# Per-batch weight loads into a ring of three, and four column strips of the array for the first conditioning step

## The chip, the cores and the metric

The kernel runs on one core of one Trainium2 chip. The metric is the device time of one execution in microseconds (us), median of several runs. A core has TensorE (PE in the rows; PEld is its weight load), VectorE (DVE), ScalarE (ACT), GpSimd (POOL) and SyncE (SP), which here does nothing but issue DMA transfers.

## What is computed

Two layers on 128 batches of 32 tokens of 128 features, fp32. Each layer is a conditioning step, chosen by an id of the batch, and a mixture of experts. The change touches the first conditioning step alone:

```python
def _L0_cond_ref(x, subjects, weights, b):        # weights: (16, 128, 128)
    w = weights[subjects]                         # one 128 x 128 matrix per batch
    out = jnp.einsum('bnc,bcd->bnd', x, w)
    out = out + b[subjects][:, None, :]
    return out
...
x = x + _L0_ffn_ref(_L0_cond_ref(x, itok_B_0_15, ...), ...)   # 16 experts, top 1, and a shared expert
x = x + _L1_ffn_ref(_L1_cond_ref(x, itok_B_0_8, ...), ...)    # adapter and norm; 8 experts, top 2, shared
```

So each 32 tokens (one batch) are multiplied by one of 16 matrices, and which one is known only when the ids have been read.

## The kernel before

The 4096 tokens are `NG` = 8 token tiles of 512 (`GP`). A tile is `G` = 4 groups of 128 tokens, and a group is `QB` = 4 batches of `S` = 32 tokens. Every engine has a program of its own; semaphores tie them. The first stage goes through the 8 tiles, software-pipelined, in the loop `for n in range(NG + 1)` of PE (line 1165), ACT (607) and DVE (806). On PE one turn n is, in this order:

1. `x_in(n + 1)`: four transposes of the next tile's x into `PS[0]`; ACT copies them to `xT` (line 604).
2. four transposes of tile n-1's conditioned rows `condS` (a view of `t3`) into `PS[5]`; DVE adds the bias and writes `featT` (line 810).
3. the 16 batch products of tile n (lines 1183 to 1192). All 16 matrices lie in SBUF in `c0w`, fetched once by ACT's queue (line 598). PE loads 16 offsets of the tile into its registers (`values_load...`, TENSOR_LOAD, line 1183) and reads the matrix of each batch at a register's offset (line 1189). The stationary operand is the 128 x 32 piece of `xT`. Batch b of a group goes to bank `PS[1 + b]`, partitions 0 to 31, so that there are four banks, and four copies of 32 x 512 move them to the right quarter of `condS`: two by ACT (line 613), two by DVE (line 817).
4. the router's logits of tile n-1 (line 1206), and four transposes back into token rows (`PS[7]`), which ACT copies to `disp` (line 617).

After every second tile DVE finds the best expert of each token (`first_max`, lines 795 to 799). After the last, DVE scans the counts (line 850), PE ranks the tokens (lines 1236 to 1239), DVE computes `slot`, and POOL scatters the 32 groups of rows to DRAM (`rows0`, line 536). It starts only when `rows0` has been filled with zeros (semaphore `zero0`, line 529). SP fetches the first blocks of it back (line 418) when all scatters have landed (`sc0`), and the experts begin.

SP issues its transfers in one fixed order: x of tiles 0 and 1, ids, five small tables (line 374), x of the other six tiles, the shared expert's weights (377 to 379; PE waits for them as `ld_sh0`, line 1232), eight loads of the experts' `w_raw` (line 382), twelve zero fills of `rows0` (388), `w_dn` (390), 28 zero fills for layer 1 (393, 396), layer 1's tables (400 to 411), and then the wait for `sc0`. ACT and POOL split `w_raw` into two parts as the tiles go by (lines 619 to 623, 523 to 527).

Of the kernel before, what the change touches and what calls it, by code (L numbers as in the profile page):

```python
# [5 lines left out]
def adaln_moe_two_layers(  # L6
# [35 lines left out]
    ALU = mybir.AluOpType  # L42
    ACT = mybir.ActivationFunctionType
    AX = mybir.AxisListType
    ds = bass.ds
# [22 lines left out]
    G = 4  # L68
# [37 lines left out]
    with ctx:  # L106
# [35 lines left out]
        sw1h = sb("sw1h", [P, F1], fp32r)  # L142
        sw1l = sb("sw1l", [P, F1], fp32r)
        used = (2 * NG + 4 + 2) * GP + 10 * F1 + 2 * NX * ROW + 4 * H + 4 * GP + 2 * NCH * P
        sb("spare", [P, NSUB * H + E0 * (C0 * H + 2 * F0x2) - used])
# [20 lines left out]
        blk_x = [sb(f"blk_x{s}", [P, ROW]) for s in range(4)]  # L166

        act0, act1 = (a[:, C0:C1, :].rearrange("p c t -> p (c t)") for a in act)
        assert 4 * H + 2 * F0 <= (C1 - C0) * GP
# [70 lines left out]
        ld_small = sem("ld_small")  # L240
        ld_c0w = sem("ld_c0w")
        ld_tab = sem("ld_tab")
# [11 lines left out]
        dve_ready = sem("dve_ready")  # L254
        off_ready = sem("off_ready")
        pe_tab = sem("pe_tab")
# [4 lines left out]
        condA = sem("condA")  # L261
        condD = sem("condD")
        pe_ht = sem("pe_ht")
# [102 lines left out]
        def _(sp):  # L366
            sp.dma_start(acc[:, 0:G, :], x_g[0]).then_inc(x_ld[0], 16)
            sp.dma_start(w0off[:, :], subj).then_inc(ld_small, 16)
            sp.dma_start(acc[:, G:2 * G, :], x_g[1]).then_inc(x_ld[1], 16)
            sp.dma_start(subjI[:, :], subj.partition_broadcast(NSUB)).then_inc(ld_tab, 16)  # L370
            sp.dma_start(langI[:, :], lang.partition_broadcast(NLANG)).then_inc(ld_tab, 16)
            for dst, src in ((c0bs[:, :], c0_b), (gam[:, :], c1_gamma), (bet[:, :], c1_beta),
                             (rt0[:, :], f0_router), (rt1[:, :], f1_router)):
                sp.dma_start(dst, src).then_inc(ld_tab, 16)
            for g in range(2, NG):
                sp.dma_start(acc[:, g * G:(g + 1) * G, :], x_g[g]).then_inc(x_ld[g], 16)
            sp.dma_start(shg[:, :], f0_sh_gate).then_inc(ld_sh0, 16)
# [3 lines left out]
            for r in range(E0 // 2):  # L381
                sp.dma_start(w_raw[:, r * 2 * F0x2:(r + 1) * 2 * F0x2].rearrange("p (e f) -> p e f", e=2),
                             f0_gate_up[2 * r:2 * r + 2].rearrange("e p f -> p e f")).then_inc(g_ld[r], 16)

# [207 lines left out]
        def _(eng):  # L592
            sc = nc.scalar

            def cp(dst, src):
                return sc.activation(dst, src, ACT.Copy)  # L596

            eng.dma_start(c0w[:, :].rearrange("p (s h) -> p s h", s=NSUB),
                          c0_w.rearrange("s p h -> p s h")).then_inc(ld_c0w, 16)
            eng.preload_act_table(ACT.Sigmoid)  # L600
# [6 lines left out]
            for n in range(NG + 1):  # L607
                if n < NG:
                    if n + 1 < NG:
                        copy_x(n + 1)  # L610
                    for b in range(2):
                        eng.wait_ge(pe_c, QB * n + b + 1)
                        cp(condS[b * S:(b + 1) * S, :, :],
                           PS[1 + b][0:S, :].rearrange("p (i h) -> p i h", h=H)).then_inc(condA, 1)
                if n >= 1:
                    eng.wait_ge(pe_tok, n)
                    cp(disp[:, (n - 1) * G:n * G, 0:H],
                       PS[7][:, :].rearrange("p (i h) -> p i h", h=H)).then_inc(tok_done, 1)
# [143 lines left out]
        def _(dve):  # L762
# [14 lines left out]
            v.memset(a_b1[TAIL:LASTK, NCH - 1:NCH], 1.0).then_inc(dve_ready, 1)  # L777
            dve.wait_ge(ld_small, 16)
            v.tensor_scalar(w0off[:, :], w0off[:, :], float(H), None, ALU.mult).then_inc(off_ready, 1)
            dve.wait_ge(poolk, 19)  # L780
# [25 lines left out]
            for n in range(NG + 1):  # L806
                if n >= 1:
# [5 lines left out]
                                    ALU.add).then_inc(hT_done, 1)  # L813
                if n < NG:
                    for b in range(2, 4):
                        dve.wait_ge(pe_c, QB * n + b + 1)
                        v.tensor_copy(condS[b * S:(b + 1) * S, :, :],
                                      PS[1 + b][0:S, :].rearrange("p (i h) -> p i h", h=H)).then_inc(condD, 1)
                if n == 0:
# [323 lines left out]
        def _(pe):  # L1143
# [21 lines left out]
            for n in range(NG + 1):  # L1165
                if n + 1 < NG:
                    x_in(n + 1)
                if n >= 1:
                    pe.wait_ge(condA, 2 * n)
                    pe.wait_ge(condD, 2 * n)  # L1170
                    if n == 1:
# [6 lines left out]
                if n < NG:  # L1178
                    pe.wait_ge(xT_done, n + 1)
                    if n == 0:  # L1180
                        pe.wait_ge(ld_c0w, 16)
                        pe.wait_ge(off_ready, 1)
                    _, offs = nc.values_load_multi_w_load_instructions(
                        w0off[0:1, n * GB:(n + 1) * GB], engines=(mybir.EngineType.PE,), min_val=0,
                        max_val=(NSUB - 1) * H, skip_runtime_bounds_check_because="subjects are under NSUB")
# [356 lines left out]
```

## Time and profile before

| | |
|---|---|
| three runs | 533.38, 534.56, 535.95 us, median 534.56 |
| the profiled execution | 532.79 us, span 531.0 us, mean granted TensorE clock 0.939 |
| first stage, first to last batch product | 9.58 to 64.7 us |
| scatter of rows for layer 0 | 79.75 to 122.4 us |
| PE, DVE, ACT, POOL busy | 84%, 45%, 47%, 48% of the span |

The span runs from the first to the last instruction; 1.8 us lie around it. Times in the trace are from the span's start. A name ending in q (SPq, PEldq) is an engine's sequencer: register work and DMA issues. The granted clock is TensorE's share of full speed: 1.00 is 2.4 GHz, 0.50 is 1.2 GHz.

### The profile page before, as it was taken

The numbers are of one execution on the slowest core, as the hardware profiler recorded it, in microseconds if no ns is written. First come the engines' busy times: TensorE is split into PE (matmuls) and PEld (weight loads), VectorE is DVE, ScalarE is ACT, GpSimd is POOL, SyncE is SP. The second block draws the span as 40 slices with busy tenths as digits, with TensorE's granted clock in tenths as the row PEclk, the third lists the DMA queues.
The fourth block names the chain that finished last, engine by engine and source line by source line (L and its number), as shares of the span: only waits on it lengthen the run. The fifth ranks groups of instructions, "written<-read, shape, count | busy, mean of one in ns | idle before, by whom it ended". The sixth has DMA issues, their size and how long they took to land.

```text
span 531.0 us, 9984 instructions
## 1 busy us (share of the span) xinstructions
PE 447.7 (84%) x3129; PEld 384.3 (72%) x3130; DVE 240.2 (45%) x708; ACT 247.4 (47%) x593; POOL 256.3 (48%) x272
## 2 busy tenths in 40 slices
PE   6798879965999998899997879918999999999900
PEld 4698746644777775477786869908999999999800
DVE  1344486422555554244868865212333233323237
ACT  2234486202555553356456534403555555555424
POOL 3003567771555555500246777760555555655510
PEclk8989999996999999899999799977999999999965
DMA  9999921111322220800001111113234324331169
GB/s 255 398 308 356 393 63 45 55 50 46 78 71 68 78 64 8 237 10 2 11 30 42 45 51 46 55 40 100 66 116 123 107 68 141 109 79 34 35 175 307
DMA packets 66131, 57.96 MB, mean 109 GB/s; under 512 B 9485, under 2 KB 53152, under 8 KB 66099
## 3 DMA queue, kind: packets, MB, share of 16 engines
q1 hardware_dynamic: 58402, 43.99, 27.7%
q0 software_dynamic: 7168, 12.51, 7.3%
q10 hardware_dynamic: 528, 1.05, 0.5%
q8 instruction: 18, 0.29, 0.2%
q14 instruction: 15, 0.11, 0.1%
HBM read 30.28 MB, written 29.47 MB: 113 GB/s over the span
## 4 chain that ended last, share of the span: by engine, by line
PE 63%; POOL 12%; issue 12%; DVE 5%; DMA 5%; ACT 1%; POOLq 1%; SPq 0%; DVEq 0%; ACTq 0%
PE PS L1459 13%; PE PS L1145 8%; POOL rows L568 7%; PE PS L1189 6%; PE PS L1381 4%; POOL rows L536 4%; PE PS L1268 4%; PE PS L1447 4%; PE PS L1448 4%; PE PS L1449 4%; PE PS L1253 2%; PE PS L1255 2%; PE PS L1254 2%; PE PS L1368 2%; PE PS L1206 2%
## 5 line engine op out<-in xcount | busy, mean ns | idle before, releaser
L586 POOL DMA_INDIRECT back<-grp_y,grp_i x80 | 79.6, 996 | 71.9 <-DVE grp_y L1102 58.0
L568 POOL DMA_INDIRECT rows<-disp,slot x64 | 64.9, 1014 | 66.8 <-DVE slot L946 47.2
L1459 PE MATMUL PS<-w2r,act 128*128 128x128 f32 x640 | 77.7, 275 | 0.0
L1459 PEld LDWEIGHTS PS<-w2r,act 128*128 128x128 f32 x640 | 74.7, 191 | 0.0
L735 ACT ACTIVATE act<-PS,b1r 128x256 f32<-128x256 f32 x160 | 62.8, 475 | 14.5 <-PE PS L1449 14.5
L547 POOL DMA_INDIRECT back<-act,blk_i x48 | 47.0, 980 | 42.0 <-DVE act L906 21.3
L1102 DVE TENSOR_TENSOR grp_y<-PS,b2r 128x256 f32<-128x256 f32 x40 | 17.0, 425 | 89.3 <-PE PS L1459 84.4
L596 ACT ACTIVATE xh<-PS 128x256 fp32r<-128x256 f32 (+1 forms) x48 | 20.0, 418 | 74.2 <-PE PS L1145 74.2
L1447 PE MATMUL PS<-xh,w1h 128*128 128x256 f32 x160 | 48.3, 302 | 0.0
L526 POOL TENSOR_TENSOR w_gul<-w_raw,w_guh 128x512 fp32r<-128x512 f32 x16 | 21.0, 1336 | 50.1 <-ACT w_guh L596 50.1
L1448 PE MATMUL PS<-xl,w1h 128*128 128x256 f32 x160 | 44.9, 281 | 0.0
L1449 PE MATMUL PS<-xh,w1l 128*128 128x256 f32 x160 | 44.9, 281 | 0.0
L1189 PE MATMUL PS<-c0w,xT 128*32 x256 | 32.6, 291 | 7.3 <-issue 7.3
L536 POOL DMA_INDIRECT rows<-disp,slot x32 | 31.7, 990 | 13.0 <-issue 8.5
L1189 PEld LDWEIGHTS PS<-c0w,xT 128*32 128x32 f32 x256 | 29.4, 118 | 10.1 <-issue 9.0
L1417 PE MATMUL PS<-sw,act 128*128 128x128 f32 x256 | 33.6, 295 | 3.0 <-DVE acc L1036 3.0
L1417 PEld LDWEIGHTS PS<-sw,act 128*128 128x128 f32 x256 | 33.3, 212 | 3.8 <-issue 3.4
L687 ACT ACTIVATE act<-PS,sb 128x512 f32<-128x512 f32 x32 | 21.6, 688 | 26.2 <-PE PS L1344 26.1
L1268 PEld LDWEIGHTS PS<-w_dn,act 128*128 128x128 f32 x192 | 25.5, 190 | 9.7 <-issue 9.2
L1268 PE MATMUL PS<-w_dn,act 128*128 x192 | 30.1, 279 | 1.1 <-ACT act L596 1.1
L1449 PEld LDWEIGHTS PS<-xh,w1l 128*128 128x128 f32 x160 | 30.2, 189 | 0.0
L1447 PEld LDWEIGHTS PS<-xh,w1h 128*128 128x128 f32 x160 | 30.2, 189 | 0.0
(216 smaller groups left out, 946.0 us busy)
## 6 DMA issues: line engine op xcount, KB each, us to landing
rows<-zrow SPq DMA_DIRECT2D x32, 258.0 KB, 5.4
grp_x<-rows SPq DMA_DIRECT2D x40, 129.0 KB, 2.3
w_raw<-in_f_gate_up SPq DMA_DIRECT2D x8, 512.0 KB, 7.7
back<-zrow SPq DMA_DIRECT2D x8, 512.0 KB, 6.9
back<-back SPq DMA_DIRECT2D x16, 256.0 KB, 4.6
blk_x<-rows SPq DMA_DIRECT2D x48, 64.5 KB, 1.8
acc<-in_x SPq DMA_DIRECT2D x8, 256.0 KB, 5.2
y0g<-back SPq DMA_DIRECT2D x8, 256.0 KB, 3.2
```

Of the source, the lines that this page charges most:

```text
L536: gp.indirect_dma_start(rows0, bass.IndirectOffsetOnAxis(ap=slot[:, 0, t:t + 1], axis=0), disp[:, t, :], None, bounds_check=NBLKP * P - 1, ...
L547: gp.indirect_dma_start(back0, bass.IndirectOffsetOnAxis(ap=blk_i[c][:, 0:1], axis=0), blk_y[s][:, :], None, bounds_check=last_token, oob_ ...
L568: gp.indirect_dma_start(rows1, bass.IndirectOffsetOnAxis(ap=slot[:, k, t:t + 1], axis=0), disp[:, t, :], None, bounds_check=E1 * CAP - 1, ...
L586: gp.indirect_dma_start(back1, bass.IndirectOffsetOnAxis(ap=grp_i[v % NX][:, u:u + 1], axis=0), grp_y[k][:, u, :], None, bounds_check=last ...
L735: sc.activation(act[k][:, c, 0:UP], PS[1 + k * (C1 // 2) + c // 2][:, (c % 2) * UP:(c % 2 + 1) * UP], ACT.Silu, bias=b1r[e][:, c:c + 1]).t ...
L1189: last = mm(PS[1 + b][0:S, i * H:(i + 1) * H], xT[n % 2][:, t * S:(t + 1) * S], c0w[:, ds(offs[t], H)], start=True, stop=True)
L1268: last = mm(PS[4 if k == 0 else 7][:, 0:H], blk_aT[k][:, c * P:(c + 1) * P], w_dn[:, ds(off + c * H, H)], start=c == 0, stop=c == C0 - 1)
L1417: last = mm(tile(PS[4], i), tile(act[n % 2][:, c, :], i), sw2[:, c, :], start=c == 0, stop=c == C1 - 1)
L1447: mm(y, high, xh[k][:, 0:UP], start=True, stop=False)
L1448: mm(y, high, xl[k][:, 0:UP], start=False, stop=False)
L1449: last = mm(y, low, xh[k][:, 0:UP], start=False, stop=True)
L1459: last = mm(PS[5 + k][:, u * P:(u + 1) * P], act[k][:, c, u * P:(u + 1) * P], w2r[e][:, c, :], start=c == 0, stop=c == C1 - 1)
```

## The change

- `c0w` shrinks to the 16 matrices of one tile. A ring `cw` of three such buffers is made of it and of the two `act` buffers, which are free in the first stage.
- ACT no longer loads `c0w`. For every tile SP reads 16 ids into its registers and issues 16 loads of 64 KB, each from the address that its id gives (`load_cond`). A matrix is now fetched once for each batch: 128 loads instead of one. From tile 3 on SP first waits until the products of tile g-3 are done (`pe_c`).
- SP's order changes: per tile x, 16 matrices, and one load of `w_raw`; the five tables come after tile 0's matrices, the shared expert's weights after all tiles, and the zero fills behind those.
- PE reads no registers. Batch b of a group writes partitions 32b to 32b+31 of one bank (`tile_position=(0, b * S)`), b the inner loop now, and tiles alternate between `PS[1]` and `PS[2]`.
- One ACT copy of 128 x 512 takes the place of the four copies. The copy to `disp` moves from ACT to DVE, between the logits' copy and `first_max`. The multiplication of the ids on DVE (line 779) is gone.

```diff
-            c0w = sb0("c0w", [P, NSUB * H])
+            c0w = sb0("c0w", [P, GB, H])
...
+        cw = [c0w] + [a[:, :, :].rearrange("p c t -> p (c t)").rearrange("p (b h) -> p b h", h=H) for a in act]
...
         def _(sp):
-            sp.dma_start(acc[:, 0:G, :], x_g[0]).then_inc(x_ld[0], 16)
+            def load_cond(g):
+                if g >= 3:
+                    sp.wait_ge(pe_c, g - 2)
+                _, who = nc.values_load_multi_w_load_instructions(
+                    w0off[0:1, g * GB:(g + 1) * GB], engines=(mybir.EngineType.SP,), min_val=0,
+                    max_val=NSUB - 1, skip_runtime_bounds_check_because="subjects are under NSUB")
+                for b in range(GB):
+                    sp.dma_start(cw[g % 3][:, b, :], at(c0_w, who[b])).then_inc(cw_ld[g % 3], 16)
...
             sp.dma_start(w0off[:, :], subj).then_inc(ld_small, 16)
-            sp.dma_start(acc[:, G:2 * G, :], x_g[1]).then_inc(x_ld[1], 16)
+            load_x(0)
             sp.dma_start(subjI[:, :], subj.partition_broadcast(NSUB)).then_inc(ld_tab, 16)
             sp.dma_start(langI[:, :], lang.partition_broadcast(NLANG)).then_inc(ld_tab, 16)
+            sp.wait_ge(ld_small, 16)
+            load_cond(0)
             for dst, src in ((c0bs[:, :], c0_b), (gam[:, :], c1_gamma), (bet[:, :], c1_beta),
                              (rt0[:, :], f0_router), (rt1[:, :], f1_router)):
                 sp.dma_start(dst, src).then_inc(ld_tab, 16)
-            for g in range(2, NG):
-                sp.dma_start(acc[:, g * G:(g + 1) * G, :], x_g[g]).then_inc(x_ld[g], 16)
+            for g in range(1, NG):
+                load_x(g)
+                load_cond(g)
+                load_gate_up(g - 1)
+            load_gate_up(E0 // 2 - 1)
             sp.dma_start(shg[:, :], f0_sh_gate).then_inc(ld_sh0, 16)
...
-            eng.dma_start(c0w[:, :].rearrange("p (s h) -> p s h", s=NSUB),
-                          c0_w.rearrange("s p h -> p s h")).then_inc(ld_c0w, 16)
...
-                    for b in range(2):
-                        eng.wait_ge(pe_c, QB * n + b + 1)
-                        cp(condS[b * S:(b + 1) * S, :, :],
-                           PS[1 + b][0:S, :].rearrange("p (i h) -> p i h", h=H)).then_inc(condA, 1)
+                    eng.wait_ge(pe_c, n + 1)
+                    cp(t3[:, :], PS[1 + n % 2][:, :]).then_inc(condA, 1)
...
+                    dve.wait_ge(pe_tok, n)
+                    v.tensor_copy(disp[:, m * G:n * G, 0:H],
+                                  PS[7][:, :].rearrange("p (i h) -> p i h", h=H)).then_inc(tok_done, 1)
...
-                    for b in range(QB):
-                        for i in range(G):
+                    pe.wait_ge(cw_ld[n % 3], 16 * GB * (n // 3 + 1))
+                    if n >= 2:
+                        pe.wait_ge(condA, n - 1)
+                    for i in range(G):
+                        for b in range(QB):
                             t = i * QB + b
-                            last = mm(PS[1 + b][0:S, i * H:(i + 1) * H],
-                                      xT[n % 2][:, t * S:(t + 1) * S], c0w[:, ds(offs[t], H)],
-                                      start=True, stop=True)
-                        last.then_inc(pe_c, 1)
+                            last = mm(PS[1 + n % 2][b * S:(b + 1) * S, i * H:(i + 1) * H],
+                                      xT[n % 2][:, t * S:(t + 1) * S], cw[n % 3][:, t, :],
+                                      start=True, stop=True, tile_position=(0, b * S))
+                    last.then_inc(pe_c, 1)
```

On SP, before, from the last small table to the zero fills (the names are the destination and the source; x4 stands for four alike):

```order
L374 DMA rt<-in_f_router 128x8
L376 DMA acc<-in_x 128x4x128 x6
L377 DMA shg<-in_f_sh_gate 128x256
L378 DMA shu<-in_f_sh_up 128x256
L379 DMA shd<-in_f_sh_down 128x2x128
L382 DMA w_raw<-in_f_gate_up 128x2x512 x8
L388 DMA rows<-zrow 128x516 [waits poolk]
L388 DMA rows<-zrow 128x516 x11
L390 DMA w_dn<-in_f_down 128x32x128
```

On SP, after, where one tile's loads end and those of tile 3 begin (`c0w` and `act` are the ring's buffers, ISA a register operation that makes an address):

```order
L378 ISA
L378 DMA act<-in_c_w 128x128
L381 DMA w_raw<-in_f_gate_up 128x2x512
L369 DMA acc<-in_x 128x4x128
L374 TENSOR_LOAD w0off [waits pe_c]
L378 ISA
L378 DMA c0w<-in_c_w 128x128
```

Every tile now has 16 such pairs of ISA and DMA on SP, where before its share was one load of x. At the end of the eight tiles the same queue reads:

```order
L378 DMA act<-in_c_w 128x128
L381 DMA w_raw<-in_f_gate_up 128x2x512 x2
L398 DMA shg<-in_f_sh_gate 128x256
L399 DMA shu<-in_f_sh_up 128x256
L400 DMA shd<-in_f_sh_down 128x2x128
L405 DMA rows<-zrow 128x516 [waits poolk]
L405 DMA rows<-zrow 128x516 x11
L407 DMA w_dn<-in_f_down 128x32x128
```

The zero fills and all that follows them stand behind the 128 loads. On PE, before, from the end of tile 0's products to the start of tile 1's:

```order
L1189 MATMUL PS<-c0w,xT 32x128
L1196 MATMUL PS<-hot,c0bs 128x128 [waits ld_tab,dve_ready]
L1197 MATMUL PS<-hot,gam 128x128
L1198 MATMUL PS<-hot,bet 128x128
L1145 MATMUL PS<-ident,acc 128x128 [waits xT_done,x_ld2]
L1145 MATMUL PS<-ident,acc 128x128 x3
L1145 MATMUL PS<-ident,t 128x128 [waits tab_done,condD,condA]
L1145 MATMUL PS<-ident,t 128x128 x3
L1183 TENSOR_LOAD w0off [waits xT_done]
L1189 ISA
```

The same place after:

```order
L1191 MATMUL PS<-c0w,xT 32x128 x15
L1198 MATMUL PS<-hot,c0bs 128x128 [waits ld_tab,dve_ready]
L1199 MATMUL PS<-hot,gam 128x128
L1200 MATMUL PS<-hot,bet 128x128
L1151 MATMUL PS<-ident,acc 128x128 [waits xT_done,x_ld2]
L1151 MATMUL PS<-ident,acc 128x128 x3
L1151 MATMUL PS<-ident,t 128x128 [waits tab_done,condA]
L1151 MATMUL PS<-ident,t 128x128 x3
L1191 MATMUL PS<-act,xT 32x128 [waits cw_ld1,xT_done]
L1191 MATMUL PS<-act,xT 32x128 x15
```

The order of the matmuls is kept; the TENSOR_LOAD and the register operations are gone, and a wait for the ring's load (`cw_ld1`) has come in. On DVE, before, at tile 1:

```order
L810 TENSOR_TENSOR featT<-PS,c0bT 128x512 [waits pe_ht]
L817 COPY t<-PS 32x512 [waits pe_c] x2
L827 COPY lg<-PS 128x64 [waits pe_l]
L795 TENSOR_REDUCE m<-lg 128x8 [waits lg_done]
```

And after:

```order
L818 TENSOR_TENSOR featT<-PS,c0bT 128x512 [waits pe_ht]
L830 COPY lg<-PS 128x64 [waits pe_l]
L832 COPY disp<-PS 128x4x128 [waits pe_tok]
L803 TENSOR_REDUCE m<-lg 128x8 [waits lg_done]
```

Two copies of 32 x 512 have left DVE, and one of 128 x 512 stands between the logits and `first_max`.

## Rows read from the trace of the kernel before

**Rows 1.** The page's head: busy time, then slices of the span in tenths.

```profile
span 531.0 us, 9984 instructions
...
PE 447.7 (84%) x3129; PEld 384.3 (72%) x3130; DVE 240.2 (45%) x708; ACT 247.4 (47%) x593; POOL 256.3 (48%) x272
...
PEclk8989999996999999899999799977999999999965
DMA  9999921111322220800001111113234324331169
```

**Rows 2.** The chain that ended last, first 80 us: start us, us, what.

```profile
9.58 5.18 PE PS L1189 x32
...
24.12 1.96 issue
26.08 5.34 PE PS L1189 x32
...
53.39 0.84 issue
54.22 3.68 PE PS L1189 x32
...
59.81 1.24 issue
61.05 3.68 PE PS L1189 x32
64.73 0.99 PE PS L1206 x8
65.73 0.93 PE PS L1145 x8
...
67.43 1.06 PE PS L1206 x8
68.49 0.48 PE PS L1145 x4
```

**Rows 3.** SP's loads at addresses from registers: duration ns min/median/max, times.

```profile
L418 SPq DMA_DIRECT2D blk_x<-rows x48: 328/333/433, 122.4 to 198.1; - x48
L418 SPq FUSED_REGOPS  x44: 46/46/57, 126.1 to 197.9; - x44
L418 SPq MOVE blk_x<-rows x44: 29/29/29, 126.2 to 198.0; - x44
...
DMA to landing us min/median/max: 1.7/1.8/2.7
```

**Rows 4.** SP's timeline in layer 1, such loads back to back: start us, us.

```profile
385.72 0.37 SPq L443 DMA_DIRECT2D w2r<-in_f_w  x1
386.28 0.36 SPq L444 DMA_DIRECT2D b1r<-in_f_b  x1
386.83 0.34 SPq L445 DMA_DIRECT2D b2r<-in_f_b  x1
```

**Rows 5.** Register loads from SBUF on PE (TENSOR_LOAD): duration ns min/median/max.

```profile
L1183 PEldq TENSOR_LOAD <-w0off x8: 1102/1723/3240, 8.1 to 58.7; - x8
...
L1274 PEldq TENSOR_LOAD <-w_at x7: 587/1111/1117, 124.3 to 197.9; - x7
```

**Rows 6.** Timeline of the first 16 us, SP's issues and the first use of the ids.

```profile
0.81 0.44 SPq L367 DMA_DIRECT2D acc<-in_x  x1
...
1.31 0.39 SPq L368 DMA_DIRECT2D w0off<-in_subj  x1
...
3.12 0.31 SPq L374 DMA_DIRECT2D c0bs<-in_c_b  x1
...
3.51 0.31 DVE L779 TENSOR_SCALAR w0off<-w0off 1x128 int32<-1x128 int32 x1 [2.30 <-DMA w0off<-in_subj]
...
5.12 4.26 SPq L376 DMA_DIRECT2D acc<-in_x  x6
...
10.60 0.43 SPq L379 DMA_DIRECT2D shd<-in_f_sh_down  x1
11.07 4.35 SPq L382 DMA_DIRECT2D w_raw<-in_f_gate_up  x8
...
15.47 10.62 SPq L388 DMA_DIRECT2D rows<-zrow  x12
```

**Rows 7.** Busy time by stretch; the last three columns: granted clock, DMA share, GB/s.

```profile
24.00:26.00 2.00, 0.12 (x2) 0.00 (x0) 0.69 (x1) 0.37 (x1) 0.00 (x0) 1.00 1.04 393
27.00:29.00 2.00, 2.00 (x11) 1.67 (x10) 0.00 (x0) 0.59 (x1) 0.00 (x0) 0.50 1.06 369
...
122.00:126.00 4.00, 1.44 (x3) 0.86 (x4) 0.59 (x3) 0.55 (x2) 0.00 (x0) 0.50 0.29 66
```

**Rows 8.** DVE's timeline from the last tile's features to the scan.

```profile
64.77 0.68 DVE L817 COPY t<-PS 32x512 f32<-32x512 f32 x1 [0.19 <-PE PS L1189]
...
66.68 0.69 DVE L810 TENSOR_TENSOR featT<-PS,c0bT 128x512 f32<-128x512 f32 x1 [0.69 <-PE PS L1145]
68.53 0.23 DVE L827 COPY lg<-PS 128x64 f32<-128x64 f32 x1 [1.16 <-PE PS L1206]
68.79 0.29 DVE L795 TENSOR_REDUCE m<-lg 128x8 f32<-128x128 f32 x1
69.11 0.97 DVE L796 TENSOR_TENSOR t<-lg,m 128x128 f32<-128x128 f32 x1
70.12 0.29 DVE L797 TENSOR_TENSOR t<-t,revE 128x128 f32<-128x128 f32 x1
...
70.76 1.36 DVE L799 TENSOR_TENSOR mask<-t,m 128x128 bf16<-128x128 f32 x1
```

**Rows 9.** POOL's timeline, the first two scatters of rows.

```profile
79.75 1.18 POOL L536 DMA_INDIRECT rows<-disp,slot  x1 [3.56 <-ACT disp L637]
81.24 0.99 POOL L536 DMA_INDIRECT rows<-disp,slot  x1 [0.31 <-ACT disp L637]
```

**Rows 10.** SP's own waits, longest first: us in total, times, longest.

```profile
SPq L418 <- DMA rows<-disp,slot: 52.5, 1, 52.5
```

**Rows 11.** SP's timeline around the fills of layer 1 and its last table.

```profile
27.22 25.00 SPq L393 DMA_DIRECT2D rows<-zrow  x20
...
52.26 8.79 SPq L396 DMA_DIRECT2D back<-zrow  x8
...
69.42 0.43 SPq L411 DMA_DIRECT2D sb<-in_f_sh_b  x1
```

More of the change, by code:

```diff
@@ L143, in adaln_moe_two_layers @@
         sw1l = sb("sw1l", [P, F1], fp32r)
+        assert GB == NSUB
         used = (2 * NG + 4 + 2) * GP + 10 * F1 + 2 * NX * ROW + 4 * H + 4 * GP + 2 * NCH * P
@@ L166, in adaln_moe_two_layers @@
         blk_x = [sb(f"blk_x{s}", [P, ROW]) for s in range(4)]
+        cw = [c0w] + [a[:, :, :].rearrange("p c t -> p (c t)").rearrange("p (b h) -> p b h", h=H) for a in act]
+        assert C1 * GP == GB * H
         act0, act1 = (a[:, C0:C1, :].rearrange("p c t -> p (c t)") for a in act)
@@ L240, in adaln_moe_two_layers @@
         ld_small = sem("ld_small")
-        ld_c0w = sem("ld_c0w")
+        cw_ld = [sem(f"cw_ld{k}") for k in range(3)]
         ld_tab = sem("ld_tab")
@@ L261, in adaln_moe_two_layers @@
         condA = sem("condA")
-        condD = sem("condD")
         pe_ht = sem("pe_ht")
@@ L366, in _, with load_x, load_gate_up @@
         def _(sp):
-            sp.dma_start(acc[:, 0:G, :], x_g[0]).then_inc(x_ld[0], 16)
+            def load_x(g):
+                sp.dma_start(acc[:, g * G:(g + 1) * G, :], x_g[g]).then_inc(x_ld[g], 16)
+            def load_cond(g):
[6 more added lines that the diff above has]
+                    sp.dma_start(cw[g % 3][:, b, :], at(c0_w, who[b])).then_inc(cw_ld[g % 3], 16)
+            def load_gate_up(r):
+                sp.dma_start(w_raw[:, r * 2 * F0x2:(r + 1) * 2 * F0x2].rearrange("p (e f) -> p e f", e=2),
+                             f0_gate_up[2 * r:2 * r + 2].rearrange("e p f -> p e f")).then_inc(g_ld[r], 16)
             sp.dma_start(w0off[:, :], subj).then_inc(ld_small, 16)
-            sp.dma_start(acc[:, G:2 * G, :], x_g[1]).then_inc(x_ld[1], 16)
+            load_x(0)
             sp.dma_start(subjI[:, :], subj.partition_broadcast(NSUB)).then_inc(ld_tab, 16)
             sp.dma_start(langI[:, :], lang.partition_broadcast(NLANG)).then_inc(ld_tab, 16)
+            sp.wait_ge(ld_small, 16)
+            load_cond(0)
             for dst, src in ((c0bs[:, :], c0_b), (gam[:, :], c1_gamma), (bet[:, :], c1_beta),
@@ L379, in _ @@
             sp.dma_start(shd[:, :, :], f0_sh_down.rearrange("(c p) h -> p c h", p=P)).then_inc(ld_sh0, 16)
-            for r in range(E0 // 2):
-                sp.dma_start(w_raw[:, r * 2 * F0x2:(r + 1) * 2 * F0x2].rearrange("p (e f) -> p e f", e=2),
-                             f0_gate_up[2 * r:2 * r + 2].rearrange("e p f -> p e f")).then_inc(g_ld[r], 16)
             sp.wait_ge(poolk, 3)
@@ L610, in _ @@
                         copy_x(n + 1)
-                    for b in range(2):
-                        eng.wait_ge(pe_c, QB * n + b + 1)
-                        cp(condS[b * S:(b + 1) * S, :, :],
-                           PS[1 + b][0:S, :].rearrange("p (i h) -> p i h", h=H)).then_inc(condA, 1)
+                    eng.wait_ge(pe_c, n + 1)
+                    cp(t3[:, :], PS[1 + n % 2][:, :]).then_inc(condA, 1)
                 if n >= 1:
-                    eng.wait_ge(pe_tok, n)
-                    cp(disp[:, (n - 1) * G:n * G, 0:H],
-                       PS[7][:, :].rearrange("p (i h) -> p i h", h=H)).then_inc(tok_done, 1)
                     for r in split_rounds(n):
@@ L813, in _ @@
                                     ALU.add).then_inc(hT_done, 1)
[L814 to L818, printed above, removed]
                 if n == 0:
@@ L1168, in _ @@
                 if n >= 1:
-                    pe.wait_ge(condA, 2 * n)
-                    pe.wait_ge(condD, 2 * n)
+                    pe.wait_ge(condA, n)
                     if n == 1:
@@ L1179, in _ @@
                     pe.wait_ge(xT_done, n + 1)
[L1180 to L1185, printed above, removed]
-                    for b in range(QB):
-                        for i in range(G):
+                    pe.wait_ge(cw_ld[n % 3], 16 * GB * (n // 3 + 1))
[3 more added lines that the diff above has]
+                        for b in range(QB):
                             t = i * QB + b
-                            last = mm(PS[1 + b][0:S, i * H:(i + 1) * H],
-                                      xT[n % 2][:, t * S:(t + 1) * S], c0w[:, ds(offs[t], H)],
-                                      start=True, stop=True)
-                        last.then_inc(pe_c, 1)
+                            last = mm(PS[1 + n % 2][b * S:(b + 1) * S, i * H:(i + 1) * H],
+                                      xT[n % 2][:, t * S:(t + 1) * S], cw[n % 3][:, t, :],
+                                      start=True, stop=True, tile_position=(0, b * S))
+                    last.then_inc(pe_c, 1)
                 if n == 0:
```

3 lines of the change are left out of this document (removed).

## The prediction

> **What bounds the kernel now.** I read the page's head first: PE is busy for 84% of the span, and PE's clock is high in nearly all slices, while the DMA engines are full only in the first eighth [rows 1]. Then the chain that ended last, for the stage that is changed. There it stands on PE nearly throughout: the batch products (L1189) of the last two tiles take 3.68 us each, logits 0.99, transposes 0.93 (more while x is left), and gaps called "issue" of 0.84 to 1.96 us stand in front of the products [rows 2]. From the first product (9.58) to the last tile's (61.05) it is 51.5 us for seven tiles, 7.35 us a tile. The gaps belong to the register load of the offsets, 1.1 to 3.2 us on PE [rows 5]. So PE's own work and its register loads set the pace, and the loads of x are long there: SP is through with all that this stage needs at 15.4 us, when its first zero fill goes out [rows 6]. After the stage come DVE's `first_max` and scan [rows 8], then the scatter, from 79.75 us on [rows 9], and SP fetches the first blocks at 122.4 [rows 3]. SP has waited 52.5 us for that [rows 10].
>
> **What goes from PE.** The eight register loads, and products that could run side by side. If PE went on setting the pace, this would be worth a lot; the first rival says how much. But each tile's products now wait for 16 loads that SP issues one after the other, so the question is what SP needs for a tile.
>
> **SP's time for a tile.** The nearest row to the new load is that of the blocks in layer 0: 128 rows of 516 bytes from an address in a register, with one register operation and one MOVE ahead. Issue 0.333 us, register work 0.046 and 0.029 [rows 3]. Between them lies time that no duration shows. Three such loads back to back start at 385.72, 386.28 and 386.83: 0.555 us apart, of which the issue is 0.36 [rows 4], so about 0.20 goes with each for registers and the gaps. With the 0.333 of the nearest shape I take 0.54 us a load, 8.64 us for 16. The bounds are 0.41 (durations alone: 0.333 + 0.046 + 0.029) and 0.62 (an issue of 0.43, as the loads of rows 6 have while the DMA engines are full, and 0.19). The register load of 16 ids moves to SP: 1.1 to 3.2 us on PE, median 1.72, and 1.11 for the later ones, when the DMA engines were nearly idle [rows 5]. The new stage lies between, since 16 x 64 KB, 256 KB of x and 512 KB of `w_raw` make 1.8 MB in some 11 us, far under the 393 GB/s that the engines reach [rows 7]. I take 1.5. A load of x takes 0.45, one of `w_raw` 4.35 / 8 = 0.54 [rows 6]. Sum for a tile: 0.45 + 1.5 + 8.64 + 0.54 = 11.1 us. PE's work of a tile is 7.35 at most. **SP is the slower one by nearly 4 us a tile**, and it is never held by the ring: it waits for the products of tile g-3, which are two turns old by then.
>
> **When the last tile's matrices are there.** The ids were in use 2.2 us after their issue (1.31 to 3.51) [rows 6]; now they go out first, at 0.81, so 3.0. Register load 1.3: 4.3. Sixteen loads: 12.9. Five tables, 2.0 (3.12 to 5.12 before) [rows 6]: 14.9. Seven more turns of 11.13, the last without its `w_raw`: 14.9 + 77.9 - 0.5 = 92.3. The last load goes out at 91.8 and lands after 1.8 us, as the blocks do [rows 3]: 93.6. The last products began at 61.05 before [rows 2], so **they begin 32.6 us later**. The late start of tile 0 (some 15 us against 9.58) and the place of x(n+1), issued behind tile n's matrices and wanted by PE ahead of tile n's products, are covered by SP's own lag in every tile but the first.
>
> **What follows the last products.** Four small terms.
> - The products themselves. Before 3.68 us at the full clock, 5.34 at the low one (26.08 us) [rows 2]. The strips have no row; between 0.9 (four at once, 3.68 / 4) and 5.3 (no gain, low clock) I take 2.0: -1.7. The Trainium skill, TensorEngine Tiling (Array Packing), section Theoretical Speedup, gives up to 4x for a dimension of 32; by that it would be 0.9 at the full clock, and no run so far shows it.
> - The clock. After the gap of 1.96 us at 24.1 the granted clock was 0.50, and likewise in the first 4 us after the scatter [rows 2, 7]. PE will now stand still for half of every tile, so I expect 0.50 through most of the stage. That costs nothing while SP is the slower one; for the last tile it doubles logits, transposes and logits again (0.99 + 0.44 + 0.48 + 1.06 + 0.48 = 3.45 [rows 2]), until the clock is back: +2.5, bounds 0 and +4.
> - The copy to `disp` on DVE stands before the last `first_max`: 0.68 as for DVE's other copies out of PSUM, and 0.2 until PE's transposes are there [rows 8]: +0.9.
> - `L796` and `L799` took 0.97 and 1.36 us beside POOL's splitting of `w_raw`, where the same work alone takes 0.29 for `L797` [rows 8]. POOL will be further ahead: -1.0.
>
> Together +0.7, so the scatter starts 33.3 us later, at 113.0 instead of 79.75 [rows 9]. All behind it moves with it.
>
> **What is also queued behind SP's loads, and its cover.** The first zero fill goes out at 92.3 + 2 x 0.54 + 3 x 0.45 = 94.8 instead of 15.47. The twelve took 10.6 us to issue [rows 6], for 3.1 MB; at about 400 GB/s with what is queued ahead they land near 107. The scatter wants them at 113: cover 6 us. The shared expert's weights go out by 94.8 and land within some 5 us; PE wants them about 103. The rest of SP's list took 15.47 to 69.85, 54.4 us [rows 6, 11], and so ends at 149.2, or sooner, since no backlog lies ahead of it now; the blocks are fetched at 122.4 + 33.3 = 155.7. **Of the 52.5 us that SP waited, 6.5 are left**, and this margin moves with the stage. I cost these at nothing.
>
> **The sum.** 531.0 + 33.3 = 564.3 us of span, 566.1 for the profiled execution (532.79 + 33.3), and for the median of the runs, which was 1.8 above it, 534.56 + 33.3 = **568**.
>
> **Rivals.**
> 1. *PE still sets the pace, and the kernel gets faster* (chance 0.03). It needs SP under 7.35 us a tile: (7.35 - 0.45 - 1.5 - 0.54) / 16 = 0.30 us a load. Then the gaps go (about 7 us), and the products fall from about 32 to about 8 us: up to 31 off, some 4 back for the late start and `disp`, about 507. Against it: the shortest issue in the trace, without any register work, is 0.31 (the table of 16 rows at 3.12 [rows 6]), and no row at a register's address is under 0.328 [rows 3]. The Trainium skill, DMA: Bandwidth & Descriptors, section Issuing engines are not separate DMA queues, says that the time to initiate a DMA on a sequencer is usually small relative to the DMA itself. By that the tile's transfers would be the bound, not their issue: 1.8 MB at 400 GB/s is 4.5 us, less than PE's work, and the time would be this rival's. Here the trace disagrees: 64 KB at 400 GB/s are 0.16 us, and the issue takes 0.33.
> 2. *The gaps between SP's loads close* (0.07), since 16 alike follow each other: 0.41 a load, 9.0 a tile. Eight tiles save 8 x 16 x 0.13 = 16.6 us: 551. Three starts 0.555 apart [rows 4] speak against it.
> 3. *The zero fill meets the scatter* (0.12). Layer 1's fills and `w_dn`, 34 us of issue before [rows 11], now run from about 106 to 140, through the first two thirds of the scatter, which had the DMA engines to itself before. If the indirect stores slow to one and a half times in 27 us, that is +13: 581. For it: no row shows an indirect store beside full engines. Against it: POOL needs 1.3 us for one, and one is only 64 KB.
> 4. *SP's issue is dearer still* (0.04): 0.62 a load and 3 us for a register load, +10 and +10: about 588.
>
> The forecast itself has 0.74. Its own band, from 0.50 to 0.59 a load (-5 and +6) and register loads of 1.1 and 2.2 (-3 and +5), with the small terms (-4 and +4), is 559 to 577. To hold 8 in 10, the range takes in most of rival 3: **557 to 584**. It leaves out rivals 1, 2 and 4. Chances (0.5%, 2.7 us, is about what a measurement of this kernel tells from no change): faster 0.03, same 0.01, slower 0.96.
>
> **What would show it.** In the profile of the changed kernel: loads of L378 on SP from about 4 to 92 us, back to back, 0.54 apart; a wait of PE's products for a DMA in every tile, the longest in the stage; products of successive tiles 11 us apart; a granted clock near 0.5 in slices 2 to 7; one ACT copy of 128 x 512 a tile; the first scatter near 113; SP's wait for the scatter down from 52.5 to under 20 us; and from the scatter on the same times as before, all shifted alike. The forecast is wrong if the products start on `xT_done` and not on a DMA (rival 1), if the loads start 0.41 apart (2), if the scatters are further apart than 1.3 us or the first one waits for `zero0` (3).

## The result and the profile after

The changed kernel takes 565.86 us (median of four runs, 564.27 to 567.26), the kernel before 533.97 (four runs). The ratio is 1.064 with a 95% interval of 1.054 to 1.075: **slower by 32 us**, forecast 568, range 557 to 584. The profiled execution took 566.36 us, its span is 564.6.

The page's slices, against [rows 1], and the queue that SP's transfers go through, which had 58402 packets, 43.99 MB and 27.7% before:

```profile
PEclk8566566799779999989999967997899999999965
DMA  3455567999722222143000111112222433312059
...
q1 hardware_dynamic: 76834, 52.39, 32.1%
```

The granted clock stands at five to eight tenths in the first seven slices where it was eight and nine, and the DMA engines are half empty there. In the kernel before they were full in slices 1 to 5; now they are full in slices 8 to 10, when the zero fill goes out. The new loads on SP and the register load ahead of them (duration ns min/median/max), against [rows 3, 5]:

```profile
L378 SPq FUSED_REGOPS  x128: 37/37/47, 3.9 to 89.8; - x128
L378 SPq DMA_DIRECT2D act<-in_c_w x80: 332/333/1707, 16.2 to 89.9; - x80
L378 SPq DMA_DIRECT2D c0w<-in_c_w x48: 332/333/377, 4.1 to 79.1; - x48
...
DMA to landing us min/median/max: 1.7/1.9/3.2
```

```profile
L374 SPq TENSOR_LOAD <-w0off x8: 973/984/1238, 2.6 to 80.5; - x8
```

They fill SP from 4 to 90 us. SP's timeline of two tiles (start us, us), in which a merged row is a run of loads:

```profile
25.31 0.46 SPq L369 DMA_DIRECT2D acc<-in_x  x1
26.97 9.08 SPq L378 DMA_DIRECT2D act<-in_c_w  x16
36.10 0.43 SPq L381 DMA_DIRECT2D w_raw<-in_f_gate_up  x1
36.58 0.46 SPq L369 DMA_DIRECT2D acc<-in_x  x1
38.24 8.52 SPq L378 DMA_DIRECT2D c0w<-in_c_w  x16
46.82 0.43 SPq L381 DMA_DIRECT2D w_raw<-in_f_gate_up  x1
47.29 0.46 SPq L369 DMA_DIRECT2D acc<-in_x  x1
```

From one load of x to the next it is 11.3 and 10.7 us, 10.9 on average over tiles 2 to 7 (25.31 to 79.99 in five turns). PE in the same stage, what it waited for, and SP's wait for the scatter, against [rows 10]:

```profile
PE PS L1151 <- DMA acc<-in_x: 43.9, 7, 10.8
```

```profile
SPq L435 <- DMA rows<-disp,slot: 8.3, 1, 8.3
```

PE waits 43.9 us for SP's queue, and SP waits for nothing in the stage, not for the ring either. Its wait for the scatter, 52.5 us before, is down to 8.3. The end of the stage in the chain, against [rows 2]:

```profile
87.78 1.00 PE PS L1208 x8
88.78 0.92 PE PS L1151 x8
89.70 2.21 issue
91.91 1.93 PE PS L1191 x32
93.84 1.82 PE PS L1208 x8
95.66 1.80 PE PS L1151 x8
97.48 0.70 DVE featT L818
98.23 1.89 PE PS L1208 x8
100.12 0.95 PE PS L1151 x4
```

After 2.21 us without work the same instructions that took 1.00 and 0.92 take 1.82 and 1.80. The scatters of rows on POOL, against [rows 9]:

```profile
L553 POOL DMA_INDIRECT rows<-disp,slot x32: 977/979/1184, 111.4 to 151.6; - x32
...
DMA to landing us min/median/max: 2.5/6.9/7.9
```

Where the time came in, by the same place in both traces:

| place | before | after | shift |
|---|---|---|---|
| last tile's products begin | 61.05 | 91.91 | 30.9 |
| first scatter of rows | 79.75 | 111.40 | 31.7 |
| SP fetches the first block | 122.40 | 154.08 | 31.7 |
| layer 0's results fetched back | 211.12 | 244.34 | 33.2 |
| end of the span | 531.0 | 564.6 | 33.6 |

### The profile page after: what moved, and what is told of

Read it like the earlier page. It is cut to its first block, busy times and chain, and to the rows that moved or that the text cites. A ratio compares the mean times of both kernels' runs of the same rounds, so it can differ in the third digit from the quotient of the medians.

```text
span 564.6 us, 10219 instructions
## 1 busy us (share of the span) xinstructions
PE 450.5 (80%) x3128; PEld 382.3 (68%) x3130; DVE 233.7 (41%) x699; ACT 239.1 (42%) x576; POOL 255.6 (45%) x272
## 3 DMA queue, kind: packets, MB, share of 16 engines
HBM read 37.62 MB, written 29.47 MB: 119 GB/s over the span
## 4 chain that ended last, share of the span: by engine, by line
PE 55%; SPq 12%; issue 10%; POOL 9%; DVE 6%; DMA 4%; ACT 2%; POOLq 0%; DVEq 0%; ACTq 0%
PE PS L1461 13%; SPq L378 8%; PE PS L1151 7%; POOL rows L585 5%; PE PS L1383 4%; POOL rows L553 4%; PE PS L1270 4%; PE PS L1449 3%; PE PS L1450 3%; PE PS L1451 3%; PE PS L1255 2%; PE PS L1257 2%; PE PS L1256 2%; PE PS L1370 2%; PE PS L1165 1%
## 5 line engine op out<-in xcount | busy, mean ns | idle before, releaser
L1151 PE MATMUL PS<-ident,acc 128*128 128x128 f32 x64 | 13.7, 354 | 45.4 <-DMA acc<-in_x 43.9
L1151 PEld LDWEIGHTS PS<-ident,acc 128*128 128x128 f32 x64 | 9.5, 179 | 50.4 <-DMA acc<-in_x 47.8
L553 POOL DMA_INDIRECT rows<-disp,slot x32 | 31.7, 992 | 18.4 <-ACT disp L647 9.8
L1419 PE MATMUL PS<-sw,act 128*128 128x128 f32 x256 | 37.2, 315 | 3.0 <-DVE acc L1042 3.0
L1419 PEld LDWEIGHTS PS<-sw,act 128*128 128x128 f32 x256 | 36.8, 231 | 3.8 <-issue 3.4
```

The source lines that it names most:

```text
L553: gp.indirect_dma_start(rows0, bass.IndirectOffsetOnAxis(ap=slot[:, 0, t:t + 1], axis=0), disp[:, t, :], None, bounds_check=NBLKP * P - 1, ...
L1151: return nc.tensor.transpose(dst, src, ident[0:k, 0:k])
L1419: last = mm(tile(PS[4], i), tile(act[n % 2][:, c, :], i), sw2[:, c, :], start=c == 0, stop=c == C1 - 1)
```

## The experiments

My theory: the number of SP's issues carries the whole loss; the strips' gain is real but hidden behind it. Rivals: the 7.3 MB more that are fetched (37.62 MB read from HBM against 30.28 by the pages); the place of x in the queue; a cost of the strips. Each run is timed against the kernel before of the same comparison. Eight of them had it at 533.5 or 534.7 us. In the other four (eleven copies on ACT, twice; PE kept busy, twice) the traces show engines standing still for tens of us in places, and the kernel before took 600.4 and 591.7 us. Of these four only the ratios are read, and the traces ahead of the first such place.

### The ring alone

```diff
 # on the kernel before: ring, SP's order and loads as in the change;
 # products in four banks one after the other, four copies, as before
-                                      xT[n % 2][:, t * S:(t + 1) * S], c0w[:, ds(offs[t], H)],
+                                      xT[n % 2][:, t * S:(t + 1) * S], cw[n % 3][:, t, :],
```

> The kernel before with the ring and SP's new order alone: the products stay one after the other in four banks, with four copies, though with fixed operands. My theory: the ring carries the whole loss, the strips are hidden behind SP in seven of eight tiles. Only the last tile's products show: 5.3 us at the low clock against 1.9, so 569 us (566 + 3.4), PE's turn at the low clock of about 9.5 us still below SP's 10.9. Rival: the strips hide a real loss on PE at the low clock, and without them every tile is longer by 1 us or more: 574 or above.

Measured: 565.28 us (563.44 to 566.72), ratio 1.060 (1.053 to 1.066), the same as the full change. Its chain at the last tile:

```profile
92.91 3.61 PE PS L1196 x32
```

The products took 3.61 us, not the 5.3 that I expected: the last products ran at the full clock here, with 0.83 granted from 60 to 100 us against 0.59 in the changed kernel, and the first scatter began at 111.53 against 111.40. So the strips, with the copies that come with them, bring nothing in the changed kernel, not even at its last tile.

### The strips alone

```diff
 # on the kernel before; all 16 matrices stay in c0w; the selection by id is left out
-                            last = mm(PS[1 + b][0:S, i * H:(i + 1) * H],
-                                      xT[n % 2][:, t * S:(t + 1) * S], c0w[:, ds(offs[t], H)],
+                            last = mm(PS[1 + n % 2][b * S:(b + 1) * S, i * H:(i + 1) * H],
+                                      xT[n % 2][:, t * S:(t + 1) * S], c0w[:, t * H:(t + 1) * H],
+                                      ..., tile_position=(0, b * S))
```

> The kernel before with the strips alone: all matrices stay in SBUF, one fetch, the products in four strips with one copy, and operands fixed when the program is built; the selection by id is left out. It prices what the change gains on PE if SP is not in the way. My first rival in the prediction: gaps of 7 us gone and products from 32 to 8 us, 534 - 31 = 503 to 507. If the strips do not run side by side, only the gaps go: 527. If another engine or the full DMA engines take over: 515 to 527.

Measured: 510.80 us (507.74 to 514.38), ratio 0.960 (0.953 to 0.968). From its chain, with 3.68 in [rows 2]:

```profile
16.51 1.01 PE PS L1179 x32
17.52 1.01 PE PS L1196 x8
```

Side by side the products take 1.01 us instead of 3.68, both at the full clock: 3.6 times. The Trainium skill, TensorEngine Tiling (Array Packing), section Theoretical Speedup, has up to 4x, and this agrees. Without SP in the way the stage gains 23 us, and the time is the first rival's 507 but for 4 us. PE's register loads are gone in this run too, and a run below shows that moving them alone is worth 8 us; the strips and their copies make the rest. The fast end is thus real; what closed it is where the matrices come from.

### The same bytes in one load a tile

```diff
-                for b in range(GB):
-                    sp.dma_start(cw[g % 3][:, b, :], at(c0_w, who[b])).then_inc(cw_ld[g % 3], 16)
+                sp.dma_start(cw[g % 3][:, :, :], c0_w.rearrange("s p h -> p s h")).then_inc(cw_ld[g % 3], 16)
```

> The changed kernel, but each tile's 1 MB of matrices comes in one load (all 16 matrices in their order), not in 16; the bytes are the same. The selection by the batch's id is left out. SP then needs about 0.45 + 0.45 + 0.54 = 1.4 us a tile instead of 10.9. My theory (the number of SP's issues is the bound): the stage falls back to what PE or the transfers need, about 5 us a tile, so some 45 to 60 us less than the changed kernel, 505 to 520 us. Rival, the bytes: refetching 8.4 MB is what costs, then it stays at 560 or above. Rival, one load for all is itself slow to issue (2048 rows of 512 bytes), and holds SP for several us a tile: between, 530 to 550.

Measured: 526.07 us (524.58 to 528.65), ratio 0.988 (0.981 to 0.995): 40 us less than the changed kernel with the same bytes, and even less than the kernel before. So the bytes are not the cause of the 32 us. Whether they are free is another matter: with one fetch of the matrices, in the run above, it was 511, though that run differs in more than the bytes. But it is 6 us above my band, and SP's rows tell why:

```profile
L377 SPq DMA_DIRECT2D w_raw<-in_f_gate_up x8: 472/4122/4442, 8.4 to 45.4; - x8
```

The load of `w_raw` behind each such load took 4.1 us to issue instead of 0.43. Here the DMA engines are full (share 0.97 of the first 60 us, 308 GB/s, against 0.60 at most in any turn of the changed kernel's first 90). Full engines alone don't do this: before, the eight loads of `w_raw` took 4.35 / 8 = 0.54 us each in their full stretch [rows 6]. That points at the load of 2048 rows just ahead as what holds the next issue up; a tile takes some 6 us (10.20 to 33.67 for four). In kind this is the third outcome that I had named, though 526 lies between its 530 to 550 and my 505 to 520.

### Addresses fixed when the program is built

```diff
-                _, who = nc.values_load_multi_w_load_instructions(w0off[...], engines=(SP,), ...)
+                who = list(range(GB))
```

> The changed kernel with its 16 loads a tile, but from addresses fixed when the program is built (matrices 0 to 15 for every tile): no register load of the ids on SP and no register operations. The selection by id is left out. My theory: a load falls from 0.52 us (start to start) to about 0.38, and the register load of 1.0 goes: a tile's turn on SP from 10.9 to about 7.1 us, so 566 - 7 x 3.8 - 3 = 536. If only the register load mattered, 558. If the issue were not the bound, 566.

Measured: 550.95 us (550.38 to 552.28), ratio 1.033 (1.027 to 1.040). It misses my 536 by 15 us. The rows of its loads:

```profile
L376 SPq DMA_DIRECT2D act<-in_c_w x80: 431/432/1502, 12.7 to 74.7; - x80
L376 SPq DMA_DIRECT2D c0w<-in_c_w x48: 328/432/503, 2.6 to 65.5; - x48
```

The register work is gone, but the issue itself now takes 0.432 us instead of 0.333. From start to start it is 0.47 (7.47 us for the first 16) instead of 0.51 (8.15). So what I had booked as "registers and gaps", 0.20 a load, is hardly the registers' doing: without them it is 0.05 less. A turn is 9.6 us (20.86 to 30.44), where I had 7.1.

### Six of the 16 loads from ACT's queue

```diff
+                for b in range(NA):                      # NA = 6, in ACT's program
+                    eng.dma_start(cw[g % 3][:, GB - NA + b, :], at(c0_w, who[b])).then_inc(cw_ld[g % 3], 16)
```

> The changed kernel with 6 of each tile's 16 loads issued from ACT's queue, 10 from SP's; same loads, same bytes, ids honoured. My theory (the issuing sequencer's time is the bound): SP's turn falls from 10.9 to 0.46 + 0.98 + 10 x 0.52 + 0.43 = 7.1 us, ACT's is about 1.0 + 6 x 0.52 + its own 2.3 = 6.4, so 566 - 7 x 3.8 - 3 = 536. Rival, the two queues share what makes an issue slow (or the DMA engines are what is slow for 64 KB pieces): 555 to 566.

Measured: 542.31 us (541.84 to 543.30), ratio 1.014 (1.010 to 1.019), 24 us less than the full change with the same loads and the same bytes. SP's turn:

```profile
26.25 0.46 SPq L371 DMA_DIRECT2D acc<-in_x  x1
27.90 5.41 SPq L380 DMA_DIRECT2D c0w<-in_c_w  x10
33.36 0.43 SPq L383 DMA_DIRECT2D w_raw<-in_f_gate_up  x1
33.84 0.46 SPq L371 DMA_DIRECT2D acc<-in_x  x1
```

It is 7.6 us here and 7.7 on average of five (18.62 to 56.91), not the 7.1 that I expected, and so the time misses my 536 by 6 us. The loads are still 0.50 to 0.59 us each, ACT's issue is 0.342. Two sequencers issue side by side: the bound is the sequencer. The Trainium skill, DMA: Bandwidth & Descriptors, section Issuing engines are not separate DMA queues, says that issuing from several engines saves only the sequencer's time, usually small relative to the DMA. The mechanism agrees. As to "small": one load lands 1.9 us after its issue, of which the issue is 0.33, but in a run of them a load costs the sequencer 0.54, and 64 KB at 400 GB/s are 0.16.

### Loads of x ahead of the matrices

```diff
+            load_x(1)
...
-                load_x(g)
+                if g + 1 < NG:
+                    load_x(g + 1)
                 load_cond(g)
```

> The changed kernel with each load of x issued one tile earlier, ahead of the matrices and not behind them. In the changed kernel the trace names the load of x as what PE waited for, 43.9 us in seven times. My theory: that is the place in SP's queue and not a cause; the matrices come as late as before, so 566 within 0.5%, and PE waits for the matrices now. Rival: x behind the matrices costs its landing of 3 to 4 us in every tile: 540 to 550.

Measured: 564.94 us (564.08 to 565.90), ratio 1.057 (1.052 to 1.061): the same. PE's waits in its trace:

```profile
PE PS L1193 <- issue: 26.9, 6, 4.9
PE PS L1193 <- DMA c0w<-in_c_w: 7.0, 1, 7.0
PE PS L1193 <- DMA act<-in_c_w: 6.1, 1, 6.1
```

The 43.9 us that the trace put down to the load of x now stand ahead of the products. The releaser that the trace names here is the last thing in the queue, not the cause.

### The register load moved, on the kernel before

```diff
-                    _, offs = nc.values_load_multi_w_load_instructions(...)   # ahead of tile n's products
                     ...
+                    if n + 1 < NG:
+                        offs = load_offsets(n + 1)                            # behind tile n's products
```

> The kernel before, with one thing moved: PE loads the 16 offsets of the next tile right behind the products of this one, instead of just ahead of their use. Before, gaps of 7.3 us in total stand in front of the products. If they are the register load's latency with an empty PE behind it, they go: 527. If the register load only moves its gap to the next instructions, the time stays at 533. No part is left out.

Measured: 526.97 us (526.59 to 533.70), ratio 0.989 (0.982 to 0.997). Two tiles of its chain:

```profile
27.84 3.61 PE PS L1192 x32
31.46 1.02 issue
32.48 1.03 PE PS L1211 x8
33.52 1.36 PE PS L1145 x12
34.87 3.61 PE PS L1192 x32
38.48 0.99 PE PS L1211 x8
```

The load now starts some 2 us before the products end. Where it takes 1.1 us (from 36.4, with the products' end at 38.48) it costs nothing; where it takes 3.0 (from 29.3, with their end at 31.46) a gap of 1 us is left. The first scatter began at 73.3 instead of 79.75.

### The ring filled inside SBUF

All 16 matrices are fetched once, and for each tile ACT and DVE copy eight each into a ring of two; strips, banks and the one copy out of PSUM are those of the change.

```diff
+            for b in range(lo, hi):                      # 0 to 7 on ACT, 8 to 15 on DVE
+                ins = cp(cw[n % 2][:, b, :], c0w[:, ds(offs[b - lo], H)])
+            ins.then_inc(done, 1)
```

> The four strips with fixed operands, but the ring is filled inside SBUF: all 16 matrices are fetched once, as before, and for each tile ACT and DVE copy 8 matrices each from the place that the id gives into a ring of two (the act buffers). SP's list is that of before. No part is left out. My theory: without SP's issues the gain of the strips appears. With operands fixed when built and no copies the same stage gave 511. The copies cost ACT and DVE about 8 x 0.27 + 1.0 = 3.2 us a tile beside 2 to 3 of their own, so the stage is bound by them at 5 to 6 us a tile: 515 to 525, below both kernels. Rival: the register load on ACT and DVE is as dear as on PE at its worst (3 us) and they become the bound at 8 us a tile: 535 to 545.

Measured: 519.72 us (518.36 to 521.23), ratio 0.971 (0.966 to 0.975). **It beats both kernels**, with nothing left out: 15 us under the one before (534.71 in this comparison), 46 under the changed one. Moving the register load alone, in the same comparison, gave 8 of these 15; the strips and the ring in SBUF are worth the other 7. Its rows, for the DVE copies and the register loads on ACT and DVE:

```profile
L366 DVE COPY act<-c0w x64: 211/217/1312, 8.3 to 39.4; 128x128 f32 x64
```

```profile
L360 ACTq TENSOR_LOAD <-w0off x8: 545/653/1967, 7.3 to 33.6; - x8
L360 DVEq TENSOR_LOAD <-w0off x8: 594/602/1891, 7.3 to 37.7; - x8
```

A matrix is put in its place for 0.22 us on DVE and 0.30 on ACT, on engines that were idle for over half of the stage (22.3 and 19.8 us busy of 14 to 64 us before), instead of 0.54 on a queue where each tile's 16 stand in a row.

### Eleven copies on ACT, five on DVE

> The ring filled inside SBUF, with 11 of the 16 copies of a tile on ACT and 5 on DVE, instead of 8 and 8; no part left out. In the run with 8 and 8 the chain of the stage goes through DVE's copies and register loads. If DVE is the bound there, three copies fewer (3 x 0.22 = 0.65 us a tile) bring up to 4 us: 516. If ACT becomes the bound (11 x 0.30 + 0.65 + 2.3 = 6.2 us a tile against 5.3), it is slower: 522 to 526.

> Once more the ring filled inside SBUF with 11 copies a tile on ACT and 5 on DVE, since all kernels of the earlier comparison, that of before too, stood still for tens of us in places. With 8 and 8 the kernel took 519.7. In the trace of the earlier run ACT was busy for 29.0 of 36 us of the stage (23.5 with 8 and 8) and the stage was about 1.5 us longer. So I now expect that ACT has become the bound: 520 to 523. Rival, DVE's chain: 516.

Measured: 590.99 us against 600.4 (ratio 0.984, 0.975 to 0.994), and again 585.22 against 591.7 (0.989, 0.980 to 0.999). In the traces the first scatter begins at 68.3 and 70.3 us, with eight and eight at 66.7. Neither ratio is as low as the 0.971 of eight and eight; whether the split is worse, whether ACT is then the bound, or by how much, these comparisons don't settle. They bear neither expectation out.

### PE kept busy before the last tile

```diff
+                    if n == NG - 1:
+                        keep_busy(PS[3], 3)              # and once more with 1
                     pe.wait_ge(cw_ld[n % 3], 16 * GB * (n // 3 + 1))
```

> The changed kernel with three extra fp32 matmuls of 128 x 512 on zeros on PE, ahead of the last tile's wait for its matrices, into a bank that is free. It prices the clock term of the prediction. In the changed kernel PE stands still for 2.2 us there, and what follows runs at the low clock: logits 1.82 and 1.89 us against 1.00 and 1.06, transposes 1.80 and 0.95 against 0.92 and 0.48. My theory: kept busy, PE does these at the full clock, and the scatter starts about 3 us earlier: 563. Rival: the low clock there is hidden behind DVE and POOL: 566. If the extra matmuls run past the arrival of the matrices, up to 1 us is lost of it.

> The changed kernel with one extra fp32 matmul of 128 x 512 on zeros on PE ahead of the last tile's wait (three overshot: they ended 3.6 us after they began, some 3 us after the matrices had landed). My theory: one takes 0.9 to 1.7 us and ends before the matrices land, and the clock of what follows depends on whether that is enough: 563 if PE stays at the full clock from the last products to the shared expert, 566 if not. The time from the first of the last products to the end of the last logits was 8.2 us in the changed kernel and 4.9 with three extra matmuls.

Measured: ratio 1.058 (1.052 to 1.064) with three and 1.064 (1.057 to 1.072) with one, against 1.064 for the change: no difference to be told. The chain with three:

```profile
91.88 3.62 PE PS L1165 x6
95.50 1.01 PE PS L1193 x32
96.51 0.99 PE PS L1210 x8
97.50 0.50 PE PS L1151 x4
98.02 0.69 DVE disp L832
98.71 0.61 DVE featT L818
99.36 1.06 PE PS L1210 x8
100.43 0.50 PE PS L1151 x4
```

From the first of the last products to the last logits' end it is 4.9 us at the full clock (95.50 to 100.42), and 8.2 in the changed kernel (91.91 to 100.12). The low clock costs 3.3 us there, 0.9 in the products and 2.4 in the logits and transposes. But the three extra matmuls ended 3.6 us later than the products began in the changed kernel, and the shared expert behind them fell to the low clock (6.41 us for eight pieces), so the first scatter began at 113.20 and nothing was won. With one, the last products began at 91.06 and took 1.08 us, but PE was at the low clock again from 94.16 on (transposes 1.81 us); the first scatter began at 109.93, 1.5 us earlier than in the changed kernel, 0.9 of which it already had when the products began. The ratio doesn't show it.

## Why the prediction was right

**SP's time for a load** was forecast at 0.54 us; it was 0.51 in tile 0 and 0.51 to 0.59 in the others, where a few loads took up to 1.7, and 0.54 on average of all 128. The issue was 0.333, exactly that of the row chosen [rows 3]. What it is made of was told wrongly: I booked 0.20 as registers and gaps, and with the registers gone a load was only 0.05 shorter. Rival 2, in which the gaps close to 0.41, did not come.

**The register load** was mis-sized: 0.98 us on SP against 1.5, which I had placed between PE's two rows [rows 5]. That is 0.5 in each of seven turns, 3.6 us. Two thirds of it came back, as a gap of 0.17 between the register load and the first load, which the sum had not, and as sixteen loads of 8.74 us on average against 8.64: a turn was 10.94 against 11.13.

**The last products** began at 91.9 against 93.6, a shift of 30.9 against 32.6. It is nearly all of the loss, and the run with the ring alone shows that the ring makes it.

**Behind them** the four terms gave +0.7, and 31.65 - 30.86 = +0.8 was measured. Term by term: the products 1.93 us against 3.68, -1.75 for -1.7. From their end to that of the last logits 6.28 against 3.76, +2.5 for +2.5, and by the run with the extra matmuls the low clock makes 2.4 of it. From the last logits' copy to `first_max` 1.54 (100.16 to 101.70) against 0.26, +1.3 for +0.9, since DVE's copy to `disp` waits for transposes that are at the low clock. From there to the first scatter 9.70 against 10.96, -1.3 for -1.0, most of it POOL's smaller overlap: L804 takes 0.64 against 0.97 us, L807 0.72 against 1.36.

**The total** came out closer than its parts, and that is luck. The span was forecast at 564.3 and is 564.6, but the last products were 1.7 us earlier than forecast, and 1.9 us came in behind the first scatter (31.7 to 33.6), where the forecast had nothing. From the first scatter to the end of the span it was 451.3 us before, 453.2 in the changed kernel, 451.2 with the loads of x ahead, 452.3 with the ring alone and 452.8 with the ring in SBUF. The four runs of the changed kernel alone span 562.5 to 565.5 us. So the 1.9 us are within what kernels that are alike there differ by, and nothing shows them to be the change's doing. The inner band of 559 to 577 is not the sum of its own terms either, which is 556 to 583; nothing hung on it.

**The queue behind the loads** kept its cover: SP waited 8.3 us for the scatter, forecast 6.5, and the first scatter did not wait for `zero0`: it began 1.1 us behind the last step of its slots in both traces (78.62 to 79.75, 110.27 to 111.40).

**Rival 3** did half of what it said. The fills met the scatter, and a store landed after 6.9 us instead of 2.5. But POOL issued them at the same pace: 31 steps in 40.2 us both before (79.75 to 119.92) and after (111.40 to 151.61), and the last landed in 2.45, when the fills were through. Its price was nil.

**Rival 1** had the right price for the wrong kernel: 507 against the 511 that the strips alone gave. The condition, under 0.30 us a load, is far from the 0.54 measured.

Two signs that I had named were off. PE was said to wait for the matrices; the trace named x, which stands behind them in SP's list, and moving it changed nothing. And the clock was not near 0.5 throughout but 0.50 to 0.69 in the turns from 15 to 91 us, since PE came back to the full clock within a tile in four of the seven turns (logits of 1.00 us at 87.78); in the other three it was 0.50 throughout. What is left open is where 1.5 of the 1.9 us came from, those between the first block and the fetch of layer 0's results. The granted clock of the first 18 us there was 0.75 against 0.81, and no run isolated it.

## What to carry to other kernels

Price a gather by its issues first, and then by its bytes: here 128 loads of 64 KB cost one sequencer 0.54 us each, and put a queue that had 52 us to spare on the critical path, while the DMA engines were 40% idle. If a faster step is to have its operands at fixed places, bring them there with engines that have time: copies inside SBUF at 0.22 to 0.30 us each turned a loss of 32 us into a gain of 15, half of which the register load alone gives when it is moved. Whether the strips could read each matrix at a register's offset, with no ring at all, no run shows. And before trusting the releaser that a trace names, move it: a wait for the last load in a queue can be a wait for the queue.

## What the runs showed of the hardware

- A load of 64 KB at an address held in a register took 0.333 us to issue on SP in the changed kernel, the same load at an address fixed in the program 0.432. From start to start the two differ by only 0.05 us, the other way.
- A load of registers from SBUF takes 0.98 us on SP (16 registers), 0.60 to 0.65 on DVE and ACT (eight registers), 1.1 to 3.2 on PE (16).
- One load of 1 MB in rows of 512 bytes, beside full DMA engines, made the next issue on the same queue take 4.1 us instead of 0.43. The first zero fill behind the 2 MB of `w_dn` took 8.3 us in the changed kernel and 12.6 in the one before.
- Four column strips of 32 with fp32 operands ran 3.6 times as fast as one after the other: 16 products in 1.01 us against 3.68, both at the full clock.
- Indirect stores beside full DMA engines landed after 6.9 us instead of 2.5, at an unchanged pace of issue.
